# Diagonal key tiles placed between the off-diagonal ones in a causal attention, with longer runs of values products

## The chip, the cores and the metric

One core of one Trainium2 chip runs the whole kernel. The metric is the device time of one execution in microseconds (us). Before the change the median of three runs is 1179.27 us (1178.64 to 1185.39).

## What is computed

One transformer block on T = 2048 tokens of E = 128 features: a modulated layernorm, causal attention with 16 query heads of 64 that share 4 key-value heads (rotary positions), a gated residual, a second modulated layernorm, and a mixture of 8 experts (two for each token, inner width 512).

```python
h = _layernorm(x) * (1 + ca) + sa
q, k, v = _rotary(h @ Wq + bq), _rotary(h @ Wk + bk), h @ Wv + bv
logits = einsum('bqhgd,bkhd->bhgqk', qg, k) / sqrt(64)
logits = where(causal, logits, -1e30)
w = softmax(logits, axis=-1)
x = x + ga * (einsum('bhgqk,bkhd->bqhgd', w, v) @ Wo + bo)
h = _layernorm(x) * (1 + cb) + sb
x = x + gb * experts(h)          # top 2 of 8: (silu(h@w1) * (h@w3)) @ w2, weighted
```

## The kernel before

**Tiling.** The attention goes by 4 groups (one key-value head each) and, within a group, by 8 pair-steps J (J = 0 to 31 over the kernel). A pair-step is one chunk of 512 queries (four chunks, two pair-steps each) and two heads m = 0, 1. The keys of a chunk come in tiles of 128: tile (q, r) is tile r = 0 to 3 of key chunk q. Tiles with q below the query chunk are off-diagonal and full (512 queries wide); tiles with q equal to the query chunk are diagonal and 512 - 128r wide, with a causal mask. So a pair-step of the chunks has 4, 8, 12 or 16 tiles.

**What one tile does.** TensorE computes the scores of a tile for each head with two matmuls (lines 1472 and 1474) and on the diagonal a third for the mask (1477), into one of only two PSUM banks (`SCORE_BANKS`). ScalarE takes the exponential out of the bank, off-diagonal into `full` (line 831, a ring of seven "quads" of four tiles), diagonal into `diag` (line 840). A bank can be written again when its exponential is done. TensorE then multiplies the exponentials with the values, both heads side by side as two halves of 64 columns (line 1490, which accumulates over all tiles of the pair-step). Several values products one behind the other are called a run here.

**Maxima and side work.** Ahead of a pair-step its row maxima are found with further score matmuls (lines 1443 and, for the mask, 1446), which go through a ring of four PSUM banks that VectorE empties (line 1067). Side work on TensorE is also the projections (1418), transposes (1425, 1431, 1456), row sums (1514) and the output projection (1540). GpSimd rotates the projections (699 to 706), ScalarE copies and casts (811, 850 to 852), VectorE adds and subtracts (1045 to 1064).

**Sums of exponentials.** For the denominators, quads are added up: GpSimd adds off-diagonal quads (`poolsum`, line 669) and in the second and third chunk the diagonal tiles (678); in the fourth chunk VectorE adds the third key chunk (`quadsum`, 1085) and the four diagonal tiles (`diagsum`, 1094). VectorE folds what is left (`sum`, 1109 to 1116).

**What sets the order.** A planner writes one list of steps, and every engine walks that list and does its own part of each step. `main` holds the scores, values products and `gap`s of the group with a weight each; the weights give each step a position, and side work is spread evenly over a stretch of positions by `place` (from pair-step position `lo` to `hi`); `merge` sorts all by position. Within a pair-step `main` takes the tiles by key chunk, the diagonal last. The values products of two off-diagonal tiles form a run behind the scores of the tile that follows them; a diagonal tile's come alone behind the next tile's scores:

```python
for q in range(J // PAIRS + 1):
    for r in range(TB):
        main += [("s", J, q, r, 0), ("s", J, q, r, 1)]
        if q < J // PAIRS and r % 2 == 0:
            main.append(("gap", 2.1 * len(pending)))
        else:
            main += pending
            pending = []
        ...
        pending.append(("pv", J, q, r))
```

**After the attention.** In the last group the early rows of the expert stage are sent and its weights loaded during the last pair-steps. SyncE (lines 596 to 606) fetches the first expert rows once `quadsum` of the last pair-step has freed a quad, and loads more when `diag` is free. The expert stage (lines 1574 to 1598) follows.

## Time and profile before

| | us |
|---|---|
| median of 3 runs | 1179.27 |
| span of the profiled execution | 1192.9 |
| TensorE busy (matmuls) | 1101.2 (92%) |
| VectorE busy | 850.0 (71%) |
| ScalarE busy | 551.1 (46%) |
| GpSimd busy | 587.1 (49%) |

The trace shows one execution, whose span is 1.2% over the median of the runs. Busy times are sums over the whole span; TensorE's instructions are pipelined and their ends are modelled, so the distance from one start to the next says what a matmul costs, not its listed length. PE is TensorE's matmuls, PEld its weight loads, DVE VectorE, ACT ScalarE, POOL GpSimd, SP SyncE. The group of pair-steps 8 to 15, from 296.4 to 535.8 us, is shown most often below; the next group is built alike.

### The profile page before, as it was taken

Reading aid. Unit: us, or ns where it says so; the run is one execution under the profiler, and the core shown is the slowest. Engines: PE = TensorE matmul, PEld = TensorE weight load, DVE = VectorE, ACT = ScalarE, POOL = GpSimd, SP = SyncE. Lnnn points to the kernel's source line nnn. Section 1 sums busy time; section 2 is a strip of 40 time slices with the busy share of each in tenths; the row PEclk is TensorE's granted clock in tenths of the full one; section 3 lists DMA queues with packets and bytes.
Section 4 is the critical chain, followed back from the end, with each engine's and each line's share of the span. In section 5 each row is a group of like instructions: output and inputs, shape, how many; then the busy total and the mean of one; then the engine's idle time right before and its main releaser. Section 6 shows DMA issues by size and latency. Waiting matters only on the chain.

```text
span 1192.9 us, 16695 instructions
## 1 busy us (share of the span) xinstructions
PE 1101.2 (92%) x5727; PEld 661.8 (55%) x5727; DVE 850.0 (71%) x1752; ACT 551.1 (46%) x1155; POOL 587.1 (49%) x635
## 2 busy tenths in 40 slices
PE   3799999999999999999999999999999986888993
PEld 2455555554565555545655555456555552477893
DVE  5777978777779787777797877777878785464343
ACT  2445544544455445454544454545444443553451
POOL 5544645645356456453564564635544337125441
PEclk9879999999999999999999999999999998899997
DMA  8000000000000000000000000000010003132104
GB/s 229 15 1 1 1 2 1 1 1 1 1 1 1 1 1 2 1 1 1 1 1 1 1 1 1 1 1 1 3 70 1 1 3 120 37 83 73 39 26 119
DMA packets 30017, 25.08 MB, mean 21 GB/s; under 512 B 4480, under 2 KB 25344, under 8 KB 29936
## 3 DMA queue, kind: packets, MB, share of 16 engines
q1 hardware_dynamic: 26224, 18.45, 5.5%
q0 software_dynamic: 2272, 4.72, 1.2%
q8 instruction: 47, 0.77, 0.3%
q10 hardware_dynamic: 1440, 0.85, 0.2%
q14 instruction: 34, 0.28, 0.1%
HBM read 15.62 MB, written 8.40 MB: 20 GB/s over the span
## 4 chain that ended last, share of the span: by engine, by line
PE 76%; DVE 14%; issue 3%; ACT 2%; DMA 2%; POOL 1%; another core or an unknown queue 1%; ACTq 0%; SPq 0%; DVEq 0%; POOLq 0%
PE PS L1490 19%; PE PS L1443 12%; PE PS L1472 12%; PE PS L1474 9%; PE PS L1574 3%; DVE part_max L1067 3%; PE PS L1418 3%; PE PS L1598 2%; PE PS L1540 2%; PE PS L1456 2%; PE PS L1425 2%; PE PS L1514 2%; DVE full L1085 2%; PE PS L1446 1%; PE PS L1585 1%
## 5 line engine op out<-in xcount | busy, mean ns | idle before, releaser
L1067 DVE TENSOR_REDUCE part_max<-PS 128x1 f32<-128x512 f32 (+2 forms) x576 | 340.0, 618 | 125.2 <-PE PS L1443 101.8
L831 ACT ACTIVATE full<-PS 128x512 f32<-128x512 f32 x384 | 223.5, 598 | 217.9 <-PE PS L1474 193.1
L1472 PE MATMUL PS<-store 128*128 128x512 f32 (+3 forms) x640 | 275.5, 431 | 13.0 <-issue 8.3
L1443 PE MATMUL PS<-store 128*128 128x512 f32 (+3 forms) x640 | 250.9, 417 | 8.8 <-ACT store L811 3.4
L1474 PE MATMUL PS<-store 128*128 128x512 f32 (+3 forms) x640 | 236.0, 369 | 0.0
L669 POOL TENSOR_TENSOR full<-full 128x512 f32<-128x512 f32 x120 | 155.4, 1326 | 138.6 <-PE PS L1490 137.5
L840 ACT ACTIVATE diag<-PS 128x512 f32<-128x512 f32 (+3 forms) x256 | 111.3, 441 | 209.1 <-PE PS L1477 174.6
L1443 PEld LDWEIGHTS PS<-store 128*128 128x128 f32 x640 | 119.5, 192 | 144.1 <-DVE part_max L1067 62.0
L1490 PE MATMUL PS<-full,V 128*64 128x512 f32 x768 | 194.0, 616 | 0.0
L699 POOL TENSOR_TENSOR lower<-lower 128x320 f32<-128x320 f32 x64 | 60.2, 941 | 258.6 <-DVE lower L1045 257.1
L1472 PEld LDWEIGHTS PS<-store 128*128 128x128 f32 x640 | 124.9, 195 | 89.8 <-issue 27.0
L678 POOL TENSOR_TENSOR full<-full,diag 128x512 f32<-128x512 f32 (+3 forms) x128 | 109.9, 895 | 59.8 <-ACT diag L840 53.6
L811 ACT ACTIVATE store<-PS 128x512 fp32r<-128x512 f32 (+1 forms) x192 | 92.9, 533 | 82.8 <-PE PS L1456 55.4
L1474 PEld LDWEIGHTS PS<-store 128*128 128x128 f32 x640 | 123.3, 193 | 13.1
L1490 PE MATMUL PS<-diag,V 128*64 128x256 f32 (+3 forms) x512 | 97.1, 460 | 0.0
L1490 PEld LDWEIGHTS PS<-full,V 128*64 128x64 f32 x768 | 46.5, 138 | 68.6 <-issue 66.9
L704 POOL TENSOR_TENSOR lower<-lower 128x160 f32<-128x160 f32 x128 | 75.6, 610 | 0.0
L1112 DVE TENSOR_TENSOR full<-full 128x512 f32<-128x512 f32 x92 | 72.0, 787 | 0.0
L1341 DVE TENSOR_TENSOR full<-full,PS 128x512 f32<-128x512 f32 x39 | 26.8, 687 | 63.2 <-ACT full L910 62.7
L735 POOL DMA_INDIRECT made<-lower,back_to x39 | 37.6, 963 | 58.5 <-DVE lower L1308 57.6
L1574 PE MATMUL PS<-store 128*128 x234 | 64.3, 411 | 2.1 <-issue 2.1
L706 POOL TENSOR_TENSOR lower<-lower 128x320 f32<-128x320 f32 x64 | 61.1, 955 | 5.0
(228 smaller groups left out, 1500.4 us busy)
## 6 DMA issues: line engine op xcount, KB each, us to landing
lower<-in_L_ffn_experts_w_dram SPq DMA_DIRECT2D x16, 256.0 KB, 4.3
sent<-full SPq DMA_DIRECT2D x1, 2574.0 KB, 11.9
full<-sent SPq DMA_DIRECT2D x9, 264.0 KB, 7.3
lower<-made SPq DMA_DIRECT2D x8, 256.0 KB, 4.9
full<-in_L_attn_x_dram SPq DMA_DIRECT2D x2, 512.0 KB, 7.3
out_dram<-XA SPq DMA_DIRECT2D x4, 256.0 KB, 2.7
made<-lower,back_to POOLq DMA_INDIRECT x39, 2.2
wo_sb<-in_L_attn_Wo_dram SPq DMA_DIRECT2D x1, 512.0 KB, 10.7
```

What stands on the lines that cost most here:

```text
L669: last = nc.gpsimd.tensor_tensor(full[:, a, r], full[:, a, r], full[:, b, r], ALU.add)
L678: last = nc.gpsimd.tensor_tensor(acc[:, r, r * P:BANK], acc[:, r, r * P:BANK], diag[:, m, r, r * P:BANK], ALU.add)
L704: done = link(nc.gpsimd.tensor_tensor(rs[:, :, lo:hi], qk[:, :, HALF - lo:HEAD - lo], sn, ALU.mult))
L811: nc.scalar.activation(dst, src, ACT.Copy).then_inc(ring_act, 1)
L831: nc.scalar.activation(full[:, k % QUADS, r, :], PS[:, bank, :], ACT.Exp).then_inc(probs_ready, 1)
L840: nc.scalar.activation(diag[:, m, r, r * P:BANK], PS[:, bank, r * P:BANK], ACT.Exp)\
L1067: nc.vector.reduce_max(part_max[:, t, b:b + 1], PS[:, bank, 0:width], AX.X).then_inc(ring_dve, 1)
L1443: last = nc.tensor.matmul(PS[:, bank, 0:w], QT[:, ch % 2, h, t * P:(t + 1) * P], KT[:, 0, keys:keys + w], start=True, stop=not last_bank)
L1472: nc.tensor.matmul(o, KT[:, 0, keys:keys + P], QT[:, ch % 2, h, q0:BANK], start=True, stop=False)
L1474: last = nc.tensor.matmul(o, KT[:, 1, keys:keys + P], QMT[:, h, q0:BANK], start=False, stop=q < ch)
L1490: last = nc.tensor.matmul(PS[HEAD * m:HEAD * (m + 1), AV + J % 2, q0:BANK], V[:, values(J // N_J * TILES + kt), :], pT, start=(kt == 0), s ...
L1574: last = nc.tensor.matmul(PS[:, bank + w, :], h_parts[:, q % 2, a, j * P:(j + 1) * P], parts_of[:, bass.ds(e, 1), w, part, :].rearrange("p ...
```

## The change

The tiles of a pair-step are taken in another order, the runs of values products are formed otherwise, and the sums are made of single tiles ("pieces").

- `runs_of` lists the runs of a pair-step. First chunk: two runs of two diagonal tiles. Second: four runs of one off-diagonal and one diagonal tile. Third: four runs of two off-diagonal and one diagonal. Fourth: six runs, of two off-diagonal tiles with or without a diagonal one. All products of a run come behind the scores of the next run's first tile.
- `diag_steps` goes: the additions of diagonal tiles are no longer placed as side work but stand right behind the run in `sums_after`, as are the off-diagonal sums. Each addition is one step of one tile. `diagadd` is the diagonal addition on GpSimd, now also for r = 0 to 2 in the fourth chunk, where only r = 3 stays on VectorE (`diagsum`). GpSimd's diagonal additions count on a semaphore of their own (`diag_pool`).
- ScalarE's waits before it writes a tile of `full` or `diag` go by the piece, where they went by the quad. Start and stop of the accumulation follow the new first and last tile. In the last pair-step `quadsum` still follows its values product.

```diff
@@ planner
-    def diag_steps(J):
-        if J // PAIRS == CHUNKS - 1:
-            return [("diagsum", J, m, part) for m in range(2) for part in range(2)]
-        return [("poolsum", J, m, J // PAIRS) for m in range(2)]
+    def runs_of(ch):
+
+        on = [(ch, r) for r in range(TB)]
+        off = [(q, r) for q in range(ch) for r in range(TB)]
+        if ch == 0:
+            return [on[0:2], on[2:4]]
+        runs = []
+        for r in range(TB):
+            for ahead in {1: (1,), 2: (2,), 3: (2, 2) if r % 2 else (2,)}[ch]:
+                runs.append(off[:ahead])
+                off = off[ahead:]
+            runs[-1].append(on[r])
+        assert not off
+        return runs
...
+    def diag_into(ch, r):
+
+        at = [(ch, r) in run for run in RUNS[ch]].index(True)
+        return max([q for run in RUNS[ch][:at + 1] for q, t in run if t == r and q < ch], default=0)
+
+    def sums_after(J, run):
+
+        ch = J // PAIRS
+        items = []
+        for q, r in run:
+            if 0 < q < ch:
+                kind = "quadsum" if q == CHUNKS - 2 else "poolsum"
+                items += [(kind, J, m, q, r) for m in range(2)]
+        for q, r in run:
+            if q == ch and ch == 0:
+                items += [("diagadd", J, m, r - 1) for m in range(2) if r % 2]
+            elif q == ch:
+                kind = "diagsum" if diag_into(ch, r) == CHUNKS - 2 else "diagadd"
+                items += [(kind, J, m, r) for m in range(2)]
+        return items
...
-        for q in range(J // PAIRS + 1):
-            for r in range(TB):
+        for run in RUNS[J // PAIRS]:
+            for at, (q, r) in enumerate(run):
                 main += [("s", J, q, r, 0), ("s", J, q, r, 1)]
-                if q < J // PAIRS and r % 2 == 0:
-                    main.append(("gap", 2.1 * len(pending)))
+                if at:
+                    main.append(("gap", 2.1 * at))
                 else:
                     main += pending
-                    pending = []
...
+            pending = [("pv", J, q, r) for q, r in run] + sums_after(J, run)
...
-        place(diag_steps(6) + tail_steps(6), 7.0, 7.48),
+        place(tail_steps(6), 7.15, 7.48),
...
@@ ScalarE
-                    if r == 0 and k >= QUADS:
+                    if k >= QUADS:
                         oJ, om, oq = quad_owner[k - QUADS]
...
-                    if r == 0 and J > 0:
-                        act.wait_ge(pv_done, n.at["pv", J - 1, local(J - 1), TB - 1] + 1)
+                    if J > 0:
+                        act.wait_ge(pv_done, n.at["pv", J - 1, local(J - 1), r] + 1)
...
```

How the order moves, at three places of the second group, as the built program lists each engine's instructions (line, operation, output <- inputs, partitions x elements, count of equal ones in a row).

TensorE in the last pair-step but one of that group (J = 14, fourth chunk), at the last off-diagonal and the first diagonal tiles, before:

```order
L1490 MATMUL PS<-full,V 64x512 x4
L1472 MATMUL PS<-store 128x512
L1474 MATMUL PS<-store 128x512
L1477 MATMUL PS<-causal,ident 128x128
L1472 MATMUL PS<-store 128x512
L1474 MATMUL PS<-store 128x512
L1477 MATMUL PS<-causal,ident 128x128
L1490 MATMUL PS<-full,V 64x512 x2
L1443 MATMUL PS<-store 128x128
```

and now, at the run that ends with the third diagonal tile:

```order
L1503 MATMUL PS<-store 128x512
L1505 MATMUL PS<-store 128x512
L1474 MATMUL PS<-store 128x512
L1503 MATMUL PS<-store 128x512
L1505 MATMUL PS<-store 128x512
L1521 MATMUL PS<-full,V 64x512 x4
L1521 MATMUL PS<-diag,V 64x256 x2
L1474 MATMUL PS<-store 128x512
```

(line 1472 is now 1503, 1474 is 1505, 1477 is 1508, 1443 is 1474, 1446 is 1477, 1490 is 1521, 1540 is 1571.) The products of the first diagonal tiles had runs of their own; now a diagonal tile's products stand behind those of two off-diagonal tiles (four instructions of full width are two tiles, two heads each).

TensorE in the same pair-step, at off-diagonal tiles (2, 1) and (2, 2), before:

```order
L1472 MATMUL PS<-store 128x512
L1474 MATMUL PS<-store 128x512
L1443 MATMUL PS<-store 128x512
L1472 MATMUL PS<-store 128x512
L1474 MATMUL PS<-store 128x512
L1490 MATMUL PS<-full,V 64x512 x4
L1443 MATMUL PS<-store 128x384
L1446 MATMUL PS<-causal,ident 128x128
L1443 MATMUL PS<-store 128x512
L1472 MATMUL PS<-store 128x512
```

and now, at the same tiles:

```order
L1503 MATMUL PS<-store 128x512
L1505 MATMUL PS<-store 128x512
L1503 MATMUL PS<-store 128x512
L1505 MATMUL PS<-store 128x512
L1503 MATMUL PS<-store 128x512
L1505 MATMUL PS<-store 128x512
L1503 MATMUL PS<-store 128x512
L1505 MATMUL PS<-store 128x512
L1474 MATMUL PS<-store 128x128
L1477 MATMUL PS<-causal,ident 128x128
```

The scores of two tiles, two heads each, now stand back to back, where a run and two maxima stood between the tiles.

GpSimd, the sums around the end of J = 13 and the start of J = 14, before:

```order
L669 TENSOR_TENSOR full<-full 128x512 x8
L678 TENSOR_TENSOR full<-full,diag 128x512
L678 TENSOR_TENSOR full<-full,diag 128x384
L678 TENSOR_TENSOR full<-full,diag 128x256
L678 TENSOR_TENSOR full<-full,diag 128x128
L678 TENSOR_TENSOR full<-full,diag 128x512
L678 TENSOR_TENSOR full<-full,diag 128x384
L678 TENSOR_TENSOR full<-full,diag 128x256
L678 TENSOR_TENSOR full<-full,diag 128x128
```

and now:

```order
L697 TENSOR_TENSOR full<-full 128x512 x4
L709 TENSOR_TENSOR full<-full,diag 128x256 x2
L697 TENSOR_TENSOR full<-full 128x512 x4
L709 TENSOR_TENSOR full<-full,diag 128x128 x2
L709 TENSOR_TENSOR full<-full,diag 128x512 x2
L697 TENSOR_TENSOR full<-full 128x512 x4
L709 TENSOR_TENSOR full<-full,diag 128x384 x2
L697 TENSOR_TENSOR full<-full 128x512 x4
L709 TENSOR_TENSOR full<-full,diag 128x256 x2
```

(669 is now 697, 678 is 709.) A whole quad was added at a time, the diagonal's eight additions together; now each pair of heads' tiles is added behind its run, and additions of diagonal tiles of the fourth chunk stand in GpSimd's queue too.

## Rows read from the trace of the kernel before

**Rows 1.** The page, parts 1 and 4: engines' busy time; chain by engine, by line.

```profile
PE 1101.2 (92%) x5727; PEld 661.8 (55%) x5727; DVE 850.0 (71%) x1752; ACT 551.1 (46%) x1155; POOL 587.1 (49%) x635
...
PE 76%; DVE 14%; issue 3%; ACT 2%; DMA 2%; POOL 1%; another core or an unknown queue 1%; ACTq 0%; SPq 0%; DVEq 0%; POOLq 0%
PE PS L1490 19%; PE PS L1443 12%; PE PS L1472 12%; PE PS L1474 9%; PE PS L1574 3%; DVE part_max L1067 3%; PE PS L1418 3%; PE PS L1598 2%; PE PS L1540 2%; PE PS L1456 2%; PE PS L1425 2%; PE PS L1514 2%; DVE full L1085 2%; PE PS L1446 1%; PE PS L1585 1%
```

**Rows 2.** Windows: stretch, length, engines' busy time (instructions), PEclk, DMA share, GB/s.

```profile
296.40:535.80 239.40, 235.79 (x1218) 133.33 (x1216) 185.34 (x346) 115.99 (x256) 125.83 (x136) 1.00 0.00 1
982.70:1021.00 38.30, 28.36 (x88) 11.30 (x87) 22.41 (x38) 14.16 (x24) 24.22 (x24) 0.78 0.29 98
```

**Rows 3.** Timeline of TensorE: start, length, line, output <- inputs, shape.

```profile
432.21 1.94 PE L1490 MATMUL PS<-full,V 128*64 128x512 f32 x8
434.07 0.73 PE L1443 MATMUL PS<-store 128*128 128x512 f32 x2
434.65 0.39 PE L1472 MATMUL PS<-store 128*128 128x512 f32 x1
...
437.25 0.39 PE L1474 MATMUL PS<-store 128*128 128x512 f32 x1
437.48 0.40 PE L1443 MATMUL PS<-store 128*128 128x512 f32 x1
437.80 1.94 PE L1490 MATMUL PS<-full,V 128*64 128x512 f32 x8
...
445.84 1.08 PE L1490 MATMUL PS<-diag,V 128*64 128x512 f32 x4
446.85 0.50 PE L1443 MATMUL PS<-store 128*128 128x512 f32 x1
```

**Rows 4.** Timeline of TensorE with its wait in brackets.

```profile
506.24 0.40 PE L1472 MATMUL PS<-store 128*128 128x512 f32 x1
...
507.15 0.50 PE L1472 MATMUL PS<-store 128*128 128x512 f32 x1 [0.28 <-ACT full L831]
```

**Rows 5.** Windows: the first of four stretches, and the sum of the four.

```profile
366.00:376.00 10.00, 9.98 (x45) 4.62 (x44) 9.96 (x19) 3.35 (x8) 4.58 (x6) 1.00 0.01 2
...
sum 35.00, PE 34.70 PEld 17.30 DVE 34.79 ACT 15.25 POOL 15.56; mean PE 8.68 PEld 4.32 DVE 8.70 ACT 3.81 POOL 3.89
```

**Rows 6.** Lines by form: busy us, mean ns of one; then idle time before it.

```profile
L1112 DVE TENSOR_TENSOR full<-full 128x512 f32<-128x512 f32 x92 | 72.0, 787 | 0.0
...
L678 POOL TENSOR_TENSOR full<-full,diag 128x512 f32<-128x512 f32 x32 | 41.0, 1281 | 59.8 <-ACT diag L840 53.6 <-issue 4.9 <-POOL lower L706 1.0
...
L678 POOL TENSOR_TENSOR full<-full,diag 128x384 f32<-128x384 f32 x32 | 32.9, 1028 | 0.0
...
L678 POOL TENSOR_TENSOR full<-full,diag 128x256 f32<-128x256 f32 x32 | 24.2, 757 | 0.0
...
L1094 DVE TENSOR_TENSOR full<-full,diag 128x512 f32<-128x512 f32 x14 | 10.2, 727 | 0.0
...
L1094 DVE TENSOR_TENSOR full<-full,diag 128x256 f32<-128x256 f32 x14 | 7.8, 556 | 0.0
L1094 DVE TENSOR_TENSOR full<-full,diag 128x384 f32<-128x384 f32 x14 | 7.6, 545 | 0.0
```

**Rows 7.** One line's instructions: duration ns least/median/most.

```profile
L1112 DVE TENSOR_TENSOR full<-full x92: 673/681/1580, 122.7 to 993.2; 128x512 f32<-128x512 f32 x92
```

**Rows 8.** Chain of waits in the last pairs: start, us, what it was.

```profile
1003.38 9.92 another core or an unknown queue
```

**Rows 9.** SyncE's waits: line, released by, us in total, times, longest.

```profile
SPq L602 <- DVE full L1085: 12.4, 1, 12.4
```

**Rows 10.** Windows of the pair-steps J = 11, 13 and 15.

```profile
353.90:379.40 25.50, 24.76 (x123) 13.25 (x120) 22.89 (x44) 11.99 (x29) 14.29 (x19) 1.00 0.00 1
415.60:451.20 35.60, 35.57 (x166) 19.42 (x165) 30.67 (x61) 16.69 (x39) 22.79 (x28) 1.00 0.00 1
495.90:535.80 39.90, 39.62 (x188) 19.37 (x186) 30.89 (x56) 21.23 (x46) 24.53 (x24) 1.00 0.00 1
```

More of the change, by code:

```diff
@@ L133, in tail_steps @@
         return steps + ([("out", J // PAIRS)] if J % PAIRS == PAIRS - 1 else [])
-    def diag_steps(J):
-        if J // PAIRS == CHUNKS - 1:
-            return [("diagsum", J, m, part) for m in range(2) for part in range(2)]
-        return [("poolsum", J, m, J // PAIRS) for m in range(2)]
+    def runs_of(ch):
[11 more added lines that the diff above has]
+        return runs
+    RUNS = [runs_of(ch) for ch in range(CHUNKS)]
+    ORDER = [[tile for run in runs for tile in run] for runs in RUNS]
+    def diag_into(ch, r):
[15 more added lines that the diff above has]
+        return items
     main = []
@@ L223, in sums_of_last @@
         for p, x in order:
-            if x[0] in ("poolsum", "quadsum") and x[1] == end - 1:
+            if x[0] in ("poolsum", "quadsum", "diagadd", "diagsum") and x[1] == end - 1:
                 continue
@@ L1483, in step @@
                     need(probs_ready, n.at["s", J, q, r, 1] + 1)
-                    if q == 0 and r == 0 and J >= 2:
+                    if (q, r) == ORDER[ch][0] and J >= 2:
                         need(attn_ready, n.at["norm", J - 2] + 1)
```

114 lines of the change are left out of this document (56 added, 58 removed).

## The prediction

> **What bounds the kernel now.** I read the page's busy times first, then the chain that ended last: TensorE is busy for 92% of the span, and 76% of the chain is its work, with the values products of line 1490 as the largest single line [rows 1]. Both shares mix stages, so I went on to windows, one for each query group. In the second group (296.4 to 535.8 us, which the third repeats) TensorE is busy for 235.8 of 239.4 us at full clock, VectorE for 185.3, GpSimd for 125.8, ScalarE for 116.0 [rows 2]. TensorE is the bound there, so what an order change is worth must be read from where one matmul starts and the next one starts, not from busy time (ends are modelled). The last pair of heads is another stage: from 982.7 to 1021.0 us TensorE works for only 28.4 of 38.3 us and its clock averages 0.78 of full speed, that is, part of it stood at the lower of its two levels [rows 2].
>
> **What a run of values products costs.** The scores and maxima use the array as 128x128, the values products as two halves of 64 columns. Starts show what each change between them costs [rows 3]. A run of two tiles goes from 432.21 to 434.07, 1.86 us; a single tile of the same width from 445.84 to 446.85, 1.01 us. So a second tile adds 0.85 us, and a run costs 0.16 us by itself. At the entry, the maximum matmul ahead of a run holds the array from 437.48 to 437.80, 0.32 us, where the matmuls ahead of it follow each other by 0.23: another 0.09. At the exit, two maximum matmuls behind a run take 434.07 to 434.65, 0.58 us in place of 0.46: 0.12. Together 0.37 us for a run, however many tiles are in it.
>
> The Trainium skill has a rule for this: TensorEngine Tiling (Array Packing), Key Properties, says that changing the tiling mode drains TensorE, and in the skill's TensorE: Matmul & The Clock Gate, Step-by-step: what each phase is for, a drain is about 128 cycles. By these two pages my estimate for a run is two drains, 0.11 us at 2.4 GHz, so 9.8 us for all the runs that go, and the sum below would come out some 3 us above the time before; that is the ground of the fourth rival. The trace shows more than three times that for a run, so [rows 3] carry the sum.
>
> **The change, part by part.** *Runs.* Before, the four diagonal tiles of a pair of heads come last and each gets a run of its own. Counted in the order of the built program there are 220 runs of values products before and 128 after, with the same 320 tiles: 92 runs fewer, 92 x 0.37 = **34.0 us** less on TensorE. The lower bound is the part inside a run alone, 92 x 0.16 = 14.7 us; I take the whole, since entry and exit are read from starts in this stage.
>
> *Score tiles with no run between them.* What stood between two tiles of scores now stands there less often. From one tile to the next, 219 of 319 steps had a run in between before and 127 have one after, so 92 more steps rely on side work (maxima, projections, transposes) to cover the exponentials, since there are only two score banks. The price of a step with nothing in between: the second head's scores start at 506.24 and the next tile's at 507.15, released by the exponential of line 831 [rows 4], where two matmuls that follow each other by 0.23 us would have let it start at 506.70. That is 0.45 us. Steps with nothing between go from 9 to 28, those with a single maximum (0.23 us, so 0.22 us uncovered) from 6 to 14; the other 65 added steps have two pieces or more, which cover the 0.45. Sum: 19 x 0.45 + 8 x 0.22 = 8.6 + 1.8 = **10.4 us** lost. Bounds: nothing lost where the exponential is done sooner, and 92 x 0.45 = 41.4 us where no side work covers.
>
> *VectorE.* The maxima keep their order and number, but in four stretches of the group VectorE is already saturated, 34.79 of 35.00 us in all, 9.96 of 10 in the first [rows 5]; that is 14.6% of 239.4 us. A faster TensorE only waits there for the four ring banks. I take 14.6% of the 34.0 us as not realised: **5.0 us**. It could be nothing (a longer run lets VectorE catch up with the banks) and, at the other end, half of the saving (the second rival).
>
> *Sums.* Of the last chunk's diagonal sums three in four move from VectorE to GpSimd: 42 additions, at 1.28, 1.03 and 0.76 us on GpSimd against 0.73, 0.55 and 0.56 us on VectorE [rows 6], so 42.9 us more on GpSimd and 25.6 us less on VectorE. In single pieces, each waits for its own values product only, and the exponentials that write the same buffer wait for a piece in place of a quad. GpSimd has room: 125.8 of 239.4 us in a group [rows 2], and about 138 afterwards. So I cost this at nothing. If the cover were gone, the rotations behind an addition in GpSimd's queue would be late, then the casts of line 850 on ScalarE, and behind them the exponentials that TensorE's score banks wait for.
>
> The skill's SBUF — State Buffer, SBUF: two separate sides, speaks against this part: a GpSimd operation and a VectorE operation with two SBUF inputs exclude each other for a whole instruction. The trace agrees that VectorE's sums are longer at times: at line 1112 they take 0.787 us on average [rows 6] and 0.673 at the least [rows 7]. GpSimd's share rises by a tenth, so my estimate by that page is a tenth more of this 0.11 us, 1 us over the 92 sums of the line and a few us of VectorE time in all, where VectorE has more than that to spare outside its saturated stretches.
>
> *The last pair.* There TensorE waits for others: the chain holds 9.92 us from 1003.38 of a queue that the profile cannot name [rows 8], and SyncE waits 12.4 us for a sum of line 1085 before it fetches the first rows of the expert stage [rows 9]. Of the 92 runs 8 lie in the last two pairs; their 8 x 0.37 = **3.0 us** I count as lost.
>
> The sum, against the profiled execution's own time: 1192.9 - 34.0 + 10.4 + 5.0 + 3.0 = 1177.3, a gain of 15.6 us. The span is 13.6 us above the median of the runs, 1.2%; I carry the difference over as it is: 1179.3 - 15.6 = **1163.7 us**.
>
> **The rivals.**
> 1. *The exponentials set the pace (slower).* If each of the 92 added steps waits the whole 0.45 us, because ScalarE's copies and casts stand ahead of the exponentials in its queue, it costs 41.4 us: -34.0 + 41.4 + 5.0 + 3.0 = +15.4, **1194.7 us**. It decides once an added step loses more than 0.28 us on average (26.0 over 92). Against it: 65 of the 92 have two pieces or more between, and ScalarE is busy for 116 of 239 us.
> 2. *VectorE becomes the bound (no change).* In the second pair of each of the last three chunks VectorE is busy for 22.9 of 25.5, 30.7 of 35.6 and 30.9 of 39.9 us [rows 10]. If those pairs, and the first chunk's second pair with them, keep their length, half the saving goes: -17.0 + 10.4 + 3.0 = -3.6, **1175.7 us**. For it: the maxima come in denser bunches between longer runs, and they pass through four banks. Against it: in a window of 35.6 us with 30.7 busy there are still some 5 us.
> 3. *The cover is good (more gain).* Longer runs give VectorE time to empty the banks and single maxima cover their step: -34.0 + 8.6 = -25.4, **1153.9 us**.
> 4. *Most of the 0.37 us comes back elsewhere* (matmuls that wait for a semaphore show the same exposed start): with 0.16 us for a run, and the losses of VectorE (14.6%) and of the last pair (8 runs) with it, -14.7 + 10.4 + 2.1 + 1.3 = -0.9, **1178.4 us**. The estimate by the Trainium skill's two pages above (TensorEngine Tiling (Array Packing) and TensorE: Matmul & The Clock Gate) lies next to this one.
>
> **How the numbers follow.** The sum of the parts has 0.50, with a range of its own from 1157 to 1171. Rival 1 has 0.08, rival 2 0.20, rival 3 0.14, rival 4 0.08. A change of under 1% (11.8 us) is about what a measurement of this kernel can't tell from none, so faster means below 1167.5: rival 3 and 0.42 of the 0.50, 0.56. Slower means above 1191: 0.07 of rival 1. The rest, 0.37, is within 1%. The range that leaves out rival 1 and the far edges of the others goes from 1150 to 1180.
>
> **What would show it.** Right: a run of three full tiles takes 2.7 us from start to start; an even share of some 4 to 5 us leaves each of the first three groups' windows; TensorE's waits for the exponentials grow by about 10 us in all; the additions on GpSimd have 42 more and nobody waits for them. Wrong: waits of TensorE for VectorE's maxima that grow by more than 5 us (rival 2), waits for the exponentials by more than 25 us (rival 1), or an unchanged group length although the runs are fewer (rival 4).

## The result and the profile after

The changed kernel takes 1228.28 us (median of 4 runs, 1228.08 to 1229.69) beside 1179.6 us before: 1.041 times the time before, with a 95% interval of 1.039 to 1.044. The forecast was 1163.7 us, with a range of 1150 to 1180. The time moved by about 49 us to the other side.

The page of the profile after, parts 1 and 4 (busy time of each engine; shares of the chain that ended last):

```profile
PE 1096.3 (89%) x5727; PEld 665.5 (54%) x5727; DVE 861.0 (70%) x1710; ACT 548.9 (45%) x1155; POOL 634.2 (52%) x677
...
PE 65%; DVE 20%; issue 6%; ACT 5%; POOL 2%; DMA 1%; ACTq 0%; SPq 0%; DVEq 0%; POOLq 0%
```

Beside [rows 1] two things stand out. TensorE's part of the chain fell from 76% to 65% and VectorE's rose from 14% to 20%. And VectorE is busy for 11 us more with 42 instructions fewer, where the change took 25.6 us of additions from it by the durations of [rows 6].

Where the time came from is read by stages. Windows of the kernel after: the four query groups (the last without its last two pair-steps), then J = 30 and J = 31 (columns as in [rows 2]):

```profile
45.50:311.20 265.70, 243.19 (x1224) 140.21 (x1224) 194.25 (x349) 121.58 (x269) 142.53 (x154) 0.97 0.00 1
311.20:559.80 248.60, 235.39 (x1218) 134.50 (x1216) 187.95 (x333) 115.51 (x256) 139.22 (x149) 1.00 0.00 1
559.80:808.10 248.30, 235.44 (x1218) 134.50 (x1216) 186.87 (x333) 115.62 (x256) 139.59 (x149) 1.00 0.00 1
808.10:962.00 153.90, 145.58 (x790) 86.38 (x789) 119.28 (x220) 69.93 (x156) 75.70 (x85) 1.00 0.04 15
962.00:1030.90 68.90, 51.22 (x246) 29.53 (x245) 53.90 (x141) 23.26 (x41) 23.10 (x22) 0.88 0.00 1
1030.90:1074.60 43.70, 40.94 (x185) 18.00 (x185) 25.18 (x40) 25.00 (x43) 28.14 (x26) 1.00 0.28 92
```

The same windows of the kernel before, from a second profile of it (x18_before_again, below):

```profile
42.60:294.50 251.90, 243.78 (x1225) 138.32 (x1225) 195.89 (x359) 122.50 (x269) 132.51 (x144) 0.97 0.00 1
294.50:533.90 239.40, 235.78 (x1219) 133.25 (x1217) 185.49 (x346) 116.08 (x256) 125.96 (x136) 1.00 0.00 1
533.90:773.20 239.30, 235.69 (x1218) 133.23 (x1216) 185.58 (x345) 116.19 (x256) 125.95 (x136) 1.00 0.00 1
773.20:925.10 151.90, 148.29 (x797) 87.24 (x796) 118.08 (x223) 69.76 (x155) 73.19 (x81) 1.00 0.05 15
925.10:980.90 55.80, 49.11 (x248) 28.90 (x247) 44.28 (x141) 24.03 (x42) 17.16 (x17) 0.94 0.00 1
980.90:1025.10 44.20, 40.44 (x176) 17.10 (x176) 27.64 (x45) 25.70 (x43) 29.68 (x26) 0.96 0.28 91
```

The differences are +13.8, +9.2, +9.0, +2.0, +13.1 and -0.5 us, together 46.6 of the 49.7 us between the two spans (2.9 lie ahead of the first group). So the loss has two main seats: each of the first three groups is 9 us longer or more, and J = 30 alone costs 13 us. The first six pair-steps of the last group lose only 2.0 us. In J = 30 TensorE's granted clock averages 0.88 after and 0.94 before, that is, more of the stretch is at the lower level, and its matmuls are busy for 2.1 us more (51.22 against 49.11). In the second group TensorE's idle time rose from 3.6 to 13.2 us (length less busy time). TensorE's waits there (released by, us in all, times, longest), the first six rows after:

```profile
PE PS L1474 <- DVE part_max L1097: 2.6, 4, 1.4
PE PS L1545 <- DVE full L1147: 2.4, 3, 1.1
PE PS L1503 <- ACT full L860: 2.0, 7, 0.4
PE PS L1487 <- DVEq L1105: 1.5, 2, 0.9
PE PS L1449 <- DVE part_max L1097: 1.2, 2, 1.0
PE PS L1462 <- DVE part_max L1097: 1.0, 1, 1.0
```

Before, all such rows of that group together were 3.3 us, and none of them named the emptying of the ring (`part_max`); the largest was

```profile
PE PS L1456 <- DVEq L1075: 1.6, 2, 0.9
```

Most of the new waits are for VectorE: its maxima (1474, 1449, 1462 wait for a ring bank) and its folding of the sums ahead of the row sums (1545).

For the sizes that follow I went through TensorE's steps of the second group one by one: a start of scores, a maximum or side work counts as bound by the instruction whose semaphore it needed last when it comes less than 0.3 us behind that one's end, and what the step ahead of it took beyond the lower quarter of unbound steps between the same neighbours counts as lost. Worked out so from the two traces, the group's +9.2 us are: steps at their unbound length -6.2 (the fewer runs), scores bound by an exponential from 1.8 (22 starts) to 6.9 us (38), starts bound by VectorE's emptying of the ring from 1.0 to 8.4, row sums that wait for VectorE's folding from 0.1 to 2.9, all else -0.5. These add up to 8.6; 0.6 us is not assigned. The sizes are estimates that hang on the base: with one base for each pair of forms and widths the same traces give -4.2, +3.9, +7.6 and +2.6.

### The profile page after: what moved, and what is told of

It reads as the page before. It is cut to its first block, busy times and chain, and to the rows that moved or that the text cites. A ratio compares the mean times of both kernels' runs of the same rounds, so it can differ in the third digit from the quotient of the medians.

```text
span 1227.9 us, 17228 instructions
## 1 busy us (share of the span) xinstructions
PE 1096.3 (89%) x5727; PEld 665.5 (54%) x5727; DVE 861.0 (70%) x1710; ACT 548.9 (45%) x1155; POOL 634.2 (52%) x677
## 4 chain that ended last, share of the span: by engine, by line
PE 65%; DVE 20%; issue 6%; ACT 5%; POOL 2%; DMA 1%; ACTq 0%; SPq 0%; DVEq 0%; POOLq 0%
PE PS L1521 17%; PE PS L1474 10%; PE PS L1503 9%; PE PS L1505 7%; DVE part_max L1097 5%; DVE full L1143 3%; PE PS L1605 3%; PE PS L1571 2%; PE PS L1449 2%; PE PS L1545 2%; ACT full L860 2%; PE PS L1456 2%; PE PS L1629 2%; PE PS L1487 2%; DVE store L1083 2%
## 5 line engine op out<-in xcount | busy, mean ns | idle before, releaser
L709 POOL TENSOR_TENSOR full<-full,diag 128x512 f32<-128x512 f32 (+3 forms) x170 | 160.4, 965 | 110.2 <-PE PS L1521 92.8
L1521 PE MATMUL PS<-full,V 128*64 128x512 f32 x768 | 191.2, 612 | 0.0
L728 POOL TENSOR_TENSOR lower<-lower 128x320 f32<-128x320 f32 x64 | 57.7, 901 | 213.6 <-DVE lower L1075 212.3
L1521 PE MATMUL PS<-diag,V 128*64 128x256 f32 (+3 forms) x512 | 89.9, 440 | 0.0
L1143 DVE TENSOR_TENSOR full<-full 128x512 f32<-128x512 f32 x92 | 76.0, 833 | 3.2 <-POOL full L709 3.2
L1521 PEld LDWEIGHTS PS<-diag,V 128*64 128x64 f32 x512 | 35.6, 138 | 66.2 <-issue 64.8
L1117 DVE TENSOR_TENSOR full<-full 128x512 f32<-128x512 f32 x72 | 61.9, 919 | 13.1 <-PE PS L1521 9.4
```

What stands on the lines that cost most here:

```text
L709: last = nc.gpsimd.tensor_tensor(acc, acc, diag[:, m, r, r * P:BANK], ALU.add)
L1143: ins = nc.vector.tensor_tensor(acc[:, piece], acc[:, piece], acc[:, piece + 2], ALU.add)
L1521: last = nc.tensor.matmul(PS[HEAD * m:HEAD * (m + 1), AV + J % 2, q0:BANK], V[:, values(J // N_J * TILES + kt), :], pT, start=((q, r) == O ...
```

## The experiments

Theory A: the new sums cost the time, through GpSimd. Theory B: the new order of tiles costs it, through exponentials without cover and denser maxima. Both are measured by the same windows. A ratio is to runs of the kernel before that were taken beside it (medians 1180.7, 1177.8, 1176.3 and 1180.0 us).

### The new sums in the old order

```diff
...
-        for run in RUNS[J // PAIRS]:
-            for at, (q, r) in enumerate(run):
+        for q in range(J // PAIRS + 1):
+            for r in range(TB):
                 main += [("s", J, q, r, 0), ("s", J, q, r, 1)]
-                if at:
-                    main.append(("gap", 2.1 * at))
+                if q < J // PAIRS and r % 2 == 0:
+                    main.append(("gap", 2.1 * len(pending)))
                 else:
-                    main += pending
+                    main += pending + [y for x in pending for y in sums_after(x[1], [x[2:]])]
...
```

> The tiles and the runs of values products in the old order (220 runs), the sums in single pieces right behind their products as after the change; the fourth chunk's diagonal sums all on VectorE as before. Theory A (the new sums cost the time: GpSimd's single additions meet VectorE's and make them longer): some 15 us or more above the kernel before, 1195 or more. Theory B (the new order costs it, by score tiles with no run between them and denser maxima): within 5 us of the kernel before, 1175 to 1185.

Measured (x1_old_order): 1204.16 us (1.0215, 1.017 to 1.026). Theory A's time holds: the sums alone cost some 24 us. Its reason does not: VectorE's instructions are no longer than before (the sums of lengthening stand further below). One place where it shows is J = 11 (27.9 us in place of 25.5), where TensorE's next maximum starts 1.9 us late for want of a ring bank. GpSimd, VectorE and TensorE there (timeline; the bracket is the wait ahead):

```profile
366.04 0.88 POOL L727 TENSOR_TENSOR lower<-lower 128x320 f32<-128x320 f32 x1 [11.51 <-DVE lower L1074]
366.87 1.01 POOL L732 TENSOR_TENSOR lower<-lower 128x160 f32<-128x160 f32 x2
367.96 0.87 POOL L734 TENSOR_TENSOR lower<-lower 128x320 f32<-128x320 f32 x1
369.06 0.86 POOL L708 TENSOR_TENSOR full<-full,diag 128x128 f32<-128x128 f32 x2 [0.24 <-ACT full L859]
...
369.55 0.93 DVE L1142 TENSOR_TENSOR full<-full 128x512 f32<-128x512 f32 x1 [1.59 <-POOL full L708]
...
370.80 0.21 DVE L1077 TENSOR_TENSOR V<-PS,lower 128x64 f32<-128x64 f32 x1
...
371.06 0.51 PE L1473 MATMUL PS<-store 128*128 128x512 f32 x1 [1.73 <-DVE V L1077]
```

The last diagonal addition stands behind a rotation in GpSimd's queue, VectorE's folding waits 1.59 us for it, and the emptying of the ring bank (L1077) stands behind the folding in VectorE's. That all of the 24 us are waits of this kind was not shown.

### The diagonal sums back on VectorE

```diff
-                kind = "diagsum" if diag_into(ch, r) == CHUNKS - 2 else "diagadd"
+                kind = "diagsum" if ch == CHUNKS - 1 else "diagadd"
...
```

> The changed kernel with all diagonal sums of the fourth chunk on VectorE (42 additions taken back from GpSimd, 43 us less there, some 26 us more on VectorE), everything else as changed. Theory A: GpSimd's additions made VectorE's longer, so 1228 falls by 10 us or more although VectorE has more to do. Theory B: no change or slower, 1225 to 1240, since VectorE's maxima bind and get later.

Measured (x2_dve_diag): 1227.29 us, the same. It tells less than hoped: GpSimd is relieved of 42 additions, but VectorE has them to do (busy for 864.9 us in place of 861.0), and the two seem to cancel. The move of the fourth chunk's sums is not the loss by itself.

### The square: old and new order, with and without GpSimd's sums

```diff
-                items += [(kind, J, m, q, r) for m in range(2)]
+                items += [(kind, J, m, q, r) for m in range(2) if kind == "quadsum"]
...
-                items += [(kind, J, m, r) for m in range(2)]
+                items += [(kind, J, m, r) for m in range(2) if kind == "diagsum"]
...
```

> The changed order, with GpSimd's sums of the second to fourth chunk left out (the off-diagonal and the diagonal ones; the denominators lack them), so that no addition on GpSimd meets one on VectorE but the rotations. Theory A: the loss goes with them, 1165 to 1190. Theory B: most of it stays, 1210 to 1225.

> The kernel before (old order), with GpSimd's sums of the second to fourth chunk left out as in x3_no_pool_sums (the denominators lack them). It completes the square of old and new order with and without these sums. If the old order's whole-quad sums cost nothing (they were hidden): 1175 to 1181, and the new order alone then costs 10 us or more (1191 against it). If they cost as much as the new sums seem to (1228 against 1191): about 1145, and the sums are a price that both orders pay.

| | with GpSimd's sums | without |
|---|---|---|
| old order | 1177.8 to 1180.7 | 1170.35 |
| new order | 1228.28 | 1191.05 |

The edit of the new order is shown; the old order's leaves out the same sums. Both theories hold in part. GpSimd's sums cost 7 to 10 us in the old order and 37 us in the new one; without them the new order still costs 20.7 us. So together they cost some 27 to 30 us more than the new order alone and the old order's sums would.

### What GpSimd's sums do: place in the queue, or reading

```diff
-                        nc.gpsimd.tensor_tensor(full[:, a, r], full[:, a, r], full[:, b, r], ALU.add)\
-                          .then_inc(pool_added, 1)
+                        thrice(full[:, a, r]).then_inc(pool_added, 1)
...
-                            last = nc.gpsimd.tensor_tensor(acc, acc, diag[:, m, r, r * P:BANK], ALU.add)
+                            last = thrice(acc)
...
+            def thrice(to):
+                for _ in range(2):
+                    nc.gpsimd.memset(to, 1.0).then_inc(pool_wrote, 1)
+                    tally[0] += 1
+                    pool.wait_ge(pool_wrote, tally[0])
+                return nc.gpsimd.memset(to, 1.0)
```

> The changed kernel, where each of GpSimd's additions of the second to fourth chunk is replaced by three writes of a constant into the same tile, one after the other (the denominators are wrong): the same place in GpSimd's queue, the same waits, about as long (some 1.4 us), but nothing is read from SBUF. If what the sums cost is that a reading GpSimd instruction holds VectorE's two-input instructions up: near the kernel with no sums on GpSimd (1191), 1188 to 1203, and VectorE's additions go back to their short lengths. If it is the queue (the rotations behind the sums, the waits for the sums): 1220 to 1230.

Measured (x13_pool_writes): 1201.72 us (1.019, 1.015 to 1.023), with GpSimd busier than after (688.5 us in place of 634.2). So 26.6 of the 37 us go when GpSimd writes as long or longer but doesn't read; the other 10.7 (1201.7 less 1191.05) remain, by its place in the queues and the waits for it. VectorE's quad sums and its subtractions of the projection's parts, by line (count, busy us, mean ns, then idle ahead of them): after,

```profile
L1117 DVE TENSOR_TENSOR full<-full 128x512 f32<-128x512 f32 x72 | 61.9, 919 | 13.1 <-PE PS L1521 9.4 <-POOL full L709 3.8
L1083 DVE TENSOR_TENSOR store<-lower,store 128x256 fp32r<-128x256 f32 x64 | 52.9, 827 | 19.7 <-ACT store L881 19.7
```

with writes in place of GpSimd's sums,

```profile
L1126 DVE TENSOR_TENSOR full<-full 128x512 f32<-128x512 f32 x72 | 50.1, 751 | 31.7 <-POOL full L691 22.6 <-PE PS L1530 9.1
L1092 DVE TENSOR_TENSOR store<-lower,store 128x256 fp32r<-128x256 f32 x64 | 38.2, 598 | 20.3 <-ACT store L890 20.2
```

and before:

```profile
L1085 DVE TENSOR_TENSOR full<-full 128x512 f32<-128x512 f32 x72 | 51.4, 778 | 13.0 <-issue 5.3 <-PE PS L1490 4.0 <-remote 3.7
L1053 DVE TENSOR_TENSOR store<-lower,store 128x256 fp32r<-128x256 f32 x64 | 43.2, 674 | 23.1 <-ACT store L851 22.2
```

The same instruction takes 778 ns before, 919 after and 751 when GpSimd only writes. Summed over all of VectorE's instructions, each against the shortest of its form in the traces, the lengthening is 90 us before, 123 after, 64 with writes, 61 without GpSimd's sums. That the sums come in small pieces is not the reason: x1_old_order has the pieces and the old order, and its lengthening is 91 us. By the same count the instructions lengthened by more than 0.1 us are 145 before, 178 after and 133 in x1_old_order. The rise comes with the new order and its sums: even with the 42 moved additions back on VectorE (x2_dve_diag) the lengthening is 111 us. What the old bundles would do in the new order was not run.

The windows say where the time lies (us, as above; "no sums" is the square's second column):

| | before | after | writes | new order, no sums | old order, no sums | new sums, old order |
|---|---|---|---|---|---|---|
| first group | 251.9 | 265.7 | 256.5 | 259.6 | 251.2 | 255.9 |
| second group | 239.4 | 248.6 | 245.2 | 242.5 | 238.0 | 243.9 |
| third group | 239.3 | 248.3 | 245.0 | 242.2 | 237.9 | 243.0 |
| J = 24 to 29 | 151.9 | 153.9 | 153.2 | 150.6 | 150.1 | 155.1 |
| J = 30 | 55.8 | 68.9 | 55.7 | 52.1 | 53.4 | 56.1 |

Of what the reading costs, 13.2 us lie in J = 30 and 9.2 in the first group; in the second and third group it is some 3.4 of 9 us.

J = 30 shows the lengthening without any sum of VectorE's in the way. There VectorE normalises the rows for the experts, nine instructions of one line. After, VectorE and GpSimd (timeline):

```profile
995.51 4.97 POOL L697 TENSOR_TENSOR full<-full 128x512 f32<-128x512 f32 x4 [19.35 <-PE PS L1521]
1000.44 1.94 POOL L709 TENSOR_TENSOR full<-full,diag 128x384 f32<-128x384 f32 x2
...
995.80 7.44 DVE L980 TENSOR_SCALAR lower<-XA,moments,rstd 128x128 f32<-128x128 f32 x9
1013.73 1.32 DVE L1194 TENSOR_TENSOR lower<-wo_sb 128x48 f32<-128x48 f32 x1
```

and before:

```profile
958.18 2.39 DVE L950 TENSOR_SCALAR lower<-XA,moments,rstd 128x128 f32<-128x128 f32 x9
...
970.77 0.24 DVE L1163 TENSOR_TENSOR lower<-wo_sb 128x48 f32<-128x48 f32 x1
```

The nine take 7.44 us in place of 2.39, from 995.80 to 1003.24, while GpSimd's sums run from 995.51 to 1002.38; a small subtraction of the routing takes 1.32 in place of 0.24 while the next sums run. Taken singly, the first six of the nine each end within 0.1 us behind one of GpSimd's six additions, and the last three take 0.33 us each: one of VectorE's instructions gets through per addition. TensorE's two longest waits in J = 30 after,

```profile
PE PS L1552 <- DVE part_max L1097: 5.8, 1, 5.8
PE PS L1578 <- issue: 5.5, 1, 5.5
```

are for the transposes of the normalised rows and for the counts of the routing; before, the transposes wait 1.1 us and the counts are not in the list. With writes in place of sums J = 30 takes 55.7 us again. The same nine instructions and the three behind them are then

```profile
978.97 2.78 DVE L989 TENSOR_SCALAR lower<-XA,moments,rstd 128x128 f32<-128x128 f32 x9
981.67 1.23 DVE L989 TENSOR_SCALAR wo_sb<-XA,moments,rstd 128x128 f32<-128x128 f32 x3
```

So GpSimd's writes, which run from 978.66, hold these up too, but little: 2.78 in place of 2.39 us, and 1.23 in place of 0.84 for the three, which after run when GpSimd's additions are over.

This is the rule that the prediction took from the Trainium skill (SBUF — State Buffer, SBUF: two separate sides) and priced too low: one of the two engines holds the shared ports for a whole instruction. The page also says that a VectorE instruction with two SBUF inputs is held only against a GpSimd instruction that reads SBUF; x13_pool_writes agrees for the quad sums, which have two (751 against 919 ns).

### Exponentials

```diff
-                    nc.scalar.activation(full[:, k % QUADS, r, :], PS[:, bank, :], ACT.Exp).then_inc(probs_ready, 1)
+                    wd = BANK if J < N_J else BANK // 2
+                    nc.scalar.activation(full[:, k % QUADS, r, 0:wd], PS[:, bank, 0:wd], ACT.Exp).then_inc(probs_ready, 1)
```

> The changed kernel, with the exponentials of off-diagonal tiles taken over only 256 of the 512 columns from the second group on (the rest of the buffer holds older values), so that a score bank is free some 0.25 us sooner. The trace after shows 38 starts of scores in a group that stand directly behind the exponential, for a loss of 6.9 us against 1.9 us before. If uncovered exponentials cost that: three groups x 5 to 7 us, 1207 to 1213. If they cost nothing in the end (VectorE paces): 1224 to 1229.

Measured (x7_half_exp): 1223.85 us (1218.31 to 1228.45), between the two. The second group is 245.8 us in place of 248.6, and the starts bound by an exponential lose 3.3 in place of 6.9 us, but VectorE's part grows by 0.8: what the exponentials give back, VectorE takes in part. Which starts they are, the prediction had not seen. TensorE after, at a full tile and the diagonal tile behind it (J = 14):

```profile
512.53 0.40 PE L1503 MATMUL PS<-store 128*128 128x512 f32 x1
512.76 0.40 PE L1505 MATMUL PS<-store 128*128 128x512 f32 x1
513.43 0.33 PE L1503 MATMUL PS<-store 128*128 128x128 f32 x1 [0.28 <-ACT full L860]
513.60 0.28 PE L1505 MATMUL PS<-store 128*128 128x128 f32 x1
513.71 0.23 PE L1508 MATMUL PS<-causal,ident 128*128 128x128 bf16 x1
513.92 0.33 PE L1503 MATMUL PS<-store 128*128 128x128 f32 x1
...
514.24 0.42 PE L1474 MATMUL PS<-store 128*128 128x384 f32 x1
```

The banks alternate between the two heads, so the second head of the narrow tile (513.92) needs the full tile's second exponential, 0.6 us long, and the first head's narrow scores cover only part of it: they take 0.49 us from start to start, where the second head's take 0.32. The first head itself starts 0.67 us behind the full scores, which follow each other by 0.23. Of the 38 bound starts after, 22 are scores of diagonal tiles and lose 4.4 us; before there is none of them, since a narrow diagonal tile stood behind a diagonal one with an exponential little wider than its own.

### More side work inside the runs, and later sums

```diff
-                    main.append(("gap", 2.1 * at))
+                    main.append(("gap", 8.4))
```

> The changed kernel with the planner's gap inside a run widened (8.4 in place of 2.1 and 4.2), so that more side work stands between the tiles of a run: steps of scores with nothing between 12 in place of 28, with a single maximum 13 in place of 14. By 0.45 us a step: 16 x 0.45 = 7 us less, 1221. If the loss is in the sums and in VectorE's maxima: no change, 1226 to 1231.

Measured (x8_wide_gaps): 1237.28 us (1.050, 1.048 to 1.053), slower still. The starts bound by an exponential do lose less (3.1 us in the group), but the first chunk's pair-step J = 8 goes from 12.6 to 15.6 us and the group to 251.5. Counting steps without cover doesn't forecast the time.

```diff
-                    main.append(("gap", 2.1 * at))
+                    main += [("gap", 2.1 * at)] + later
+                    later = []
                 else:
-                    main += pending
+                    main += later + pending
+                    late_run = len(pending) and J >= PAIRS and run is not RUNS[J // PAIRS][0]
+                    later = later_of if late_run else []
+                    main += [] if late_run else later_of
-            pending = [("pv", J, q, r) for q, r in run] + sums_after(J, run)
+            pending, later_of = [("pv", J, q, r) for q, r in run], sums_after(J, run)
...
```

> The changed kernel with the sums of a run one tile of scores later in the list of steps (second to fourth chunk, but for the last run of a pair-step), so that GpSimd and VectorE seldom stand waiting for values products just issued. If the in-order wait at a sum is the price (rotations and maxima queued behind it): 1205 to 1218. If the price is that GpSimd's and VectorE's additions meet, wherever they stand: 1224 to 1232.

Measured (x6_late_sums): 1227.32 us. Inconclusive: the list changed, but each engine's own order hardly did, since few of GpSimd's and VectorE's other steps lie in between, and the second group has the same 248.6 us.

### Runs of two in the new order

```diff
-    RUNS = [runs_of(ch) for ch in range(CHUNKS)]
-    ORDER = [[tile for run in runs for tile in run] for runs in RUNS]
+    ORDER = [[tile for run in runs_of(ch) for tile in run] for ch in range(CHUNKS)]
+    RUNS = [[order[k:k + 2] for k in range(0, len(order), 2)] for order in ORDER]
```

> The changed order of the tiles, but every run of three values products cut so that all runs are of two (160 runs in place of 128); sums in single pieces behind each run. 32 runs more at 0.25 us are +8 us; score steps with nothing between 10 in place of 28, with a single maximum 26 in place of 14: -18 x 0.45 + 12 x 0.22 = -5.5 us. If the length of the runs matters only through these: 1231. If runs of three (2.3 to 2.7 us, longer than VectorE takes to empty its four banks) starve VectorE and so bring its lateness: 1205 to 1220.

Measured (x12_runs_of_two): 1211.64 us (1.028, 1.025 to 1.031), 17 us less than the change with 32 runs more. The mechanism expected isn't what the trace shows: VectorE's part in the group stays (8.1 us against 8.4). The group is 4.1 us shorter because the starts bound by exponentials lose 3.0 in place of 6.9 us, a run now standing where a diagonal tile's scores had followed a full tile's; and J = 30 is 9.0 us shorter: its sums fall elsewhere, and TensorE's waits for the transposes and the counts are 4.5 and 1.1 us in place of 5.8 and 5.5.

### VectorE's maxima, and all three suspects at once

```diff
-                    width = BANK if b < ch else (t + 1) * P
+                    width = BANK // 2 if b < ch else (t + 1) * P
```

> The changed kernel, with VectorE's maxima over full banks read over 256 of the 512 columns (the row maxima leave out the other half of each off-diagonal key chunk), so that one takes about 0.35 us in place of 0.62. In a group the trace after puts 8.4 us on starts that stand directly behind VectorE's emptying of the ring and 2.8 us ahead of the row sums, against 1.0 and 0.1 before. If VectorE's lateness is half of the loss: 4 x 8 to 10 us less, 1185 to 1197. If these waits would only be replaced by others (exponentials, GpSimd's queue): above 1210.

> The same cut of the maxima in the kernel before, the control of x9_half_max. VectorE holds TensorE up for 1 us in a group there: 1172 to 1180.

Measured: 1204.70 us in the new order (x9_half_max) and 1163.23 in the old one (x10_before_half_max). VectorE's load costs the new order 24 us, but the old one 13 to 16 as well, more than its own waits of 1 us in the second group let expect (most of it lies in the first group, 246.6 against 251.9 us, and in J = 30 and 31). So cutting VectorE's maxima closes 7 to 10 us of the 49 between the orders; the maxima by themselves don't make the difference.

> The changed kernel with all three suspects lifted at once: GpSimd's sums of the second to fourth chunk left out, VectorE's full-bank maxima over 256 columns, off-diagonal exponentials over 256 columns from the second group on. If the loss is waits for these three, the fewer runs must now show: below x17_before_all_lifted, by up to 24 to 33 us (92 runs at 0.26 to 0.36), 1125 to 1150. If the new order has a price beside them: level with it or above.

> The control of x16_all_lifted: the same three cuts in the kernel before. Without GpSimd's sums it took 1170, with the shorter maxima 1163; both and the shorter exponentials: 1150 to 1160.

The edits are those of x3_no_pool_sums, x9_half_max and x7_half_exp together, and for the old order those of x4_before_no_pool_sums with the same cuts. Measured: 1168.12 us in the new order, 1154.93 in the old one. Of the 49 us between the orders 13 remain with all three lifted, so lifting the three closes some 36. The saving of the runs is there but doesn't win: in the second group the unbound steps are 6.1 us shorter than in the control, and the remaining waits (exponentials of the diagonal tiles 3.3 against 0.4, row sums 1.2 against 0.0, VectorE 0.9, ScalarE 1.1 more) take it back, 235.2 against 234.0 us. Most of the 13 us lie in the first group (256.3 against 246.7), where the exponentials were left at full width and where the opening of the kernel is: J = 1 takes 22.2 us there in place of 16.8, and 23.0 in the kernel after in place of 17.9 in the one before. TensorE has two waits in it of 3.4 and 2.6 us ahead of line 1487 after, and one of 2.9 before; why the maxima and transposes of the opening are late was not tested.

### The old order with fewer runs

```diff
-                if q < J // PAIRS and r % 2 == 0:
+                if len(pending) < 2 and (J >= PAIRS or r):
...
-                if r == (1 if q < J // PAIRS else 0) and q > 1:
+                if r == 1 and q > 1:
```

> The kernel before with its tile order and its sums, but the diagonal's values products in runs of two: 160 runs in place of 220, and score steps with nothing between them 16 in place of 9, with a single maximum 17 in place of 6. If a run costs 0.26 us as the traces of before and after give together: -15.6 + 7 x 0.45 + 11 x 0.22 = -10.0, 1169. If every step that loses its run loses 0.45 us (Theory B at its worst): -15.6 + 27.0 = +11, 1191.

Measured (x5_diag_pairs): 1180.84 us (0.9994, 0.997 to 1.002). 60 runs fewer are worth nothing here: the second group's unbound steps are 4.4 us shorter, the starts bound by exponentials lose 2.0 more, VectorE and the row sums 2.6 more. The first chunk alone gains, 1.7 us in a group.

> x5_diag_pairs (old order and sums, the diagonal's products in runs of two) with the planner's gap inside a run 3.15 in place of 2.1, so that steps with a single maximum between are 10 in place of 17. At 0.22 us each some 1.5 us less: 1175 to 1180; more than that would say that the place of the side work matters beyond the count of such steps.

Measured (x11_pairs_gap): 1186.34 us (1.0081, 1.006 to 1.011), slower by 5 us than x5_diag_pairs, though 7 more steps had cover; again the place of the side work outweighs the count.

```diff
-                if q < J // PAIRS and r % 2 == 0:
+                if len(pending) < 2 and (J < PAIRS and r or q < J // PAIRS and r % 2 == 0):
```

> The kernel before, with the values products in runs of two in the first chunk alone (208 runs in place of 220; no further step of scores without cover). 12 runs at 0.25 to 0.36 us: 3 to 4 us less than before; the trace of x5_diag_pairs gives 1.7 us for the two pair-steps of a group, 7 us in all. So 1170 to 1176 beside 1177 to 1180 if a run that goes without taking cover away is a gain; the same as before if not.

Measured (x14_first_chunk_pairs): 1177.96 us, 0.9974 of the kernel before (0.9955 to 0.9993), above the forecast of 1170 to 1176. Merging runs where no cover goes is a gain, of some 2 to 3 us, no more. It is the only version with all of the work that beats both kernels, and by little.

### The kernel before once more

> The kernel before once more, for a second profiled execution. The first one's span, 1192.9, is 13 us above the median of its runs, and the last pair-step took 55.5 us there against 41 to 46 in all the kernels above, also in x14_first_chunk_pairs, which has the same code from the second chunk of each group on. If the 9.92 us of a queue without a name were a chance of that execution: a span of 1176 to 1183 and no such piece in the chain. If it belongs to the kernel: 1190 to 1195 again.

Measured (x18_before_again): a span of 1178.2 us, every window as in the first profile but for J = 31, 44.2 in place of 55.5 us, and no piece of a queue without a name in the chain from 960 to 1060 us. The 9.92 us of [rows 8] were a chance of that one execution, which the prediction took for a property of the stage. Carrying the whole 13.6 us between span and median over as it stood was right, though not for a reason that the prediction had.

## Why the prediction was wrong, step by step

- **What bounds the kernel.** TensorE was the bound, but with 3.6 us of slack in 239.4 the row also says that everything else already fits into it exactly. A planner's order in which all waits are hidden has more to lose by a change than to gain. The prediction read [rows 2] only one way.
- **What a run costs.** The mechanism was right. The part inside, 0.16 us, shows in full: the group's values products take 64.4 us from start to start in place of 68.2, 3.8 us for 23 runs. A run of three full tiles takes 2.73 us, as said:

```profile
480.46 1.94 PE L1521 MATMUL PS<-full,V 128*64 128x512 f32 x8
482.23 1.03 PE L1521 MATMUL PS<-diag,V 128*64 128x512 f32 x4
483.19 0.50 PE L1474 MATMUL PS<-store 128*128 128x512 f32 x1
```

  With entry and exit the unbound steps give 6.2 us in a group, 0.27 us a run, so some 25 us in place of 34.0 (17 by the other base, 4.2 us in a group). The drain that the Trainium skill gives (0.11 us a run by the prediction's estimate) is too little against both; TensorEngine Tiling (Array Packing), Key Properties, is right that a change of mode costs.
- **Score tiles with no run between.** Sized at 10.4 us; measured 5.1 us in the second group, about 20 us over four if each were like it. The step that failed here is the count from one tile to the next. A score waits for the bank of its own head two scores back, and the narrow scores of a diagonal tile behind a full tile don't cover that tile's exponential. 22 of 38 bound starts are of this kind.
- **VectorE.** 5.0 us "not realised"; measured 7.4 us of starts bound by the ring and 2.8 of row sums more than before in the second group, about 40 us over four if each were like it. Without GpSimd's sums the starts bound by the ring lose 3.6 us and the row sums 1.6, in place of 8.4 and 2.9, so the larger part is not saturation: it goes with GpSimd's sums, by longer instructions and by waits for them.
- **Sums.** "So I cost this at nothing" is the step that failed most. GpSimd had room in its own time, and that is all that the prediction asked. What its instructions do to VectorE's while they run was put at a few us, by scaling GpSimd's share by a tenth; VectorE's lengthening grew by 33 us, from 90 to 123. The share doesn't say where the additions fall, and in J = 30 they fall on instructions that TensorE waits for. The sign "nobody waits for them" failed as well: VectorE's folding does, and the pieces cost 24 us even in the old order, without longer instructions. In the new order GpSimd's sums cost 37 us in all, 27 of them by reading.
- **The last pair.** 3.0 us for runs that bring nothing; J = 30 alone cost 13, by the same meeting of engines (none of it is left with writes).
- **The rivals.** The slower rival had a chance of 0.08 and named the exponentials; by the terms here they cost some 20 us, less than the runs save, so they alone would not have made the kernel slower. The second rival named VectorE and forecast no change, since it took VectorE's time as fixed. Its sign came: TensorE's listed waits for the emptying of the ring are 18.9 us in the groups after (up to J = 29) and none before, far over the 5 us; its time did not. None of the four had GpSimd as the cause, though the prediction's sentence on the Trainium skill's page did.

Scaled from the second group to four, the terms are runs -25, exponentials +20 and VectorE +40; with J = 30's 13 that is 48, beside the measured 49. That it comes out so near is partly luck: the groups are not alike (+13.8, +9.2, +9.0, and +2.0 in the last up to J = 29). The first group's 4.6 us over the others sit in J = 1, which is 5.1 us longer than before; their cause stays open, and so does that of most of the 13 us that remain with all three suspects lifted.

## What to carry to other kernels

Where two engines read the same memory through shared ports, cost a moved or divided addition by what it meets on the other engine, instruction by instruction, and not by the free time of its own; look first at the instructions that the bounding engine waits for. In a schedule in which the bounding engine is 98% busy, count every wait that the old order hid before counting what the new one saves: a buffer that alternates between two heads ties neighbours two steps apart, so a short step behind a long one has no cover. A profile taken once can hold a wait that belongs to that execution alone; a second one is cheap.

## What the runs showed of the hardware

- While GpSimd runs additions with two SBUF inputs one behind the other, VectorE's instructions get through one at a time between them: nine `TENSOR_SCALAR` of 0.27 us (2.39 in all) take 7.44, a `TENSOR_TENSOR` of 0.24 us takes 1.32. So an instruction with one tensor as input is held as well as one with two.
- Writes of a constant by GpSimd, about as long and at the same places in its queue, don't hold up VectorE's additions with two SBUF inputs: 751 ns for the quad sums against 919. They do hold up the `TENSOR_SCALAR` with one tensor as input, by less than additions do: nine take 2.78 us in place of 2.39, three 1.23 in place of 0.84.
- VectorE's reductions out of PSUM aren't touched: 617 ns on average for the maxima after, 618 before, while the sums out of SBUF got longer.
